# Four attention layers over eight batches on one core: last layers put beside the fronts of two batches on, and the two ends paired

## The reference, cut to what matters

```python
# layer 0: self-attention over pixels through 32 latent channels, then attention to 128 concepts
th, ph, g = conv1x1(x, w_theta), conv1x1(x, w_phi), conv1x1(x, w_g)         # 32 x 1024 each
sa_out = gamma_sa * conv1x1(softmax(th.T @ ph) @ g, w_o) + x
out0 = gamma_moca * conv1x1(softmax(conv1x1(sa_out, w_theta).T @ concepts.T) @ concepts, w_o) + sa_out
# layer 1: q and k of 32 channels, v of 256
out1 = softmax(q.T @ k) @ v * gamma + out0
# layer 2: group norm, q, k, v of 256 channels, one head
out2 = proj(softmax(q.T @ k / 16) @ v) + out1
# layer 3: group norm, q, k, v of 256 channels, 8 heads of 32, layer norm over channels at the end
out3 = layer_norm(wo(softmax(q.T @ k / sqrt(32)) @ v)) * ln_gamma + ln_beta + out2
```

## Time and profile before

| | us |
|---|---|
| median of 3 runs | 3100.76 |
| the profiled execution | 3099.89 |
| its span, first to last instruction | 3097.8 |
| TensorE matmul busy | 2771.0 (89%) |
| VectorE busy | 1812.1 (58%) |
| ScalarE busy | 1214.4 (39%) |
| GpSimd busy | 917.7 (30%) |
| mean granted TensorE clock | 0.885 of 2.4 GHz |

### The profile page before, as it was taken

The page is one execution under the profiler, slowest core; times in us unless marked ns, Lnnn a source line. Parts: engine busy times, 40 slices in busy tenths (PEclk is TensorE's granted clock), DMA queues, the critical chain, the costliest instruction groups (busy, mean ns, idle before and its releaser), DMA issues.

```text
span 3097.8 us, 25573 instructions
## 1 busy us (share of the span) xinstructions
PE 2771.0 (89%) x9636; PEld 1420.5 (46%) x9636; DVE 1812.1 (58%) x1749; ACT 1214.4 (39%) x2073; POOL 917.7 (30%) x371
## 2 busy tenths in 40 slices
PE   6788999989999899988999899898999989998877
PEld 3345445544354444544445444554435444454332
DVE  3233668357673766547675475835767376653675
ACT  2222262533435243442525335253343524344146
POOL 0111071502525034330515106150152503434045
PEclk7789898988989888997989989898898988899678
DMA  1002020020100201001010202002010020100300
GB/s 53 14 0 53 2 55 1 1 68 14 41 1 11 58 14 41 1 28 41 14 41 1 68 1 55 1 1 68 14 41 1 10 59 1 41 1 29 73 8 14
DMA packets 30347, 80.44 MB, mean 26 GB/s; under 512 B 10320, under 2 KB 10448, under 8 KB 28944
## 3 DMA queue, kind: packets, MB, share of 16 engines
q1 hardware_dynamic: 28048, 70.42, 9.0%
q0 software_dynamic: 2176, 8.39, 0.8%
HBM read 11.40 MB, written 8.39 MB: 6 GB/s over the span
## 4 chain that ended last, share of the span: by engine, by line
PE 70%; DVE 16%; ACT 5%; SPq 4%; issue 2%; POOL 1%; DMA 1%; DVEq 0%; ACTq 0%; POOLq 0%
PE ps L696 13%; PE ps L549 12%; PE ps L582 9%; PE ps L568 8%; DVE nmx_b L1218 8%; PE ps L863 7%; PE ps L781 6%; SPq L406 4%; DVE accb L1380 3%; PE ps L557 3%; PE ps L638 2%; PE ps L767 2%; PE ps L778 1%; POOL accb L499 1%; PE ps L678 1%
## 5 line engine op out<-in xcount | busy, mean ns | idle before, releaser
L1082 ACT ACTIVATE prb<-ps 128x512 f32<-128x512 f32 x1024 | 561.5, 599 | 452.1 <-PE ps L582 387.9
L1218 DVE TENSOR_REDUCE nmx_b<-ps 128x1 f32<-128x1024 f32 x512 | 605.6, 1216 | 102.7 <-PE ps L568 100.6
L499 POOL TENSOR_TENSOR accb<-accb,prb 128x1024 f32<-128x1024 f32 x192 | 503.3, 2621 | 247.6 <-ACT prb L1082 242.3
L568 PE MATMUL ps<-ks,qs 96*128 96x512 f32 x960 | 441.7, 570 | 118.8 <-DVE nmx_b L1218 74.6
L1380 DVE TENSOR_TENSOR accb<-accb,prb 128x1024 f32<-128x1024 f32 x192 | 396.2, 2063 | 259.5 <-ACT prb L1082 255.4
L499 POOL TENSOR_TENSOR accb<-prb 128x1024 f32<-128x1024 f32 x32 | 96.9, 3029 | 1484.7 <-ACT prb L1082 1404.2
L696 PE MATMUL ps<-pr,h 128*128 128x512 f32 x1024 | 482.7, 596 | 1.0 <-ACT tmp L978 1.0
L582 PE MATMUL ps<-qs,ks 97*128 97x512 f32 x960 | 388.0, 472 | 10.8 <-ACT prb L1082 7.8
L568 PEld LDWEIGHTS ps<-ks,qs 96*128 96x128 f32 x960 | 206.4, 246 | 322.5 <-DVE nmx_b L1218 222.8
L950 ACT ACTIVATE pr<-ps 128x512 f32<-128x512 f32 x384 | 226.7, 599 | 218.5 <-PE ps L582 104.0
L582 PEld LDWEIGHTS ps<-qs,ks 97*128 97x128 f32 x960 | 173.0, 192 | 251.9 <-ACT prb L1082 123.4
(11 more groups left out here) (157 smaller groups left out, 2714.0 us busy)
## 6 DMA issues: line engine op xcount, KB each, us to landing
qs<-part SPq DMA_DIRECT2D x180, 128.0 KB, 2.3
ks<-part SPq DMA_DIRECT2D x180, 128.0 KB, 2.3
x_in<-in_x POOLq DMA_DIRECT2D x8, 1024.0 KB, 5.3
xd<-xm SPq DMA_DIRECT2D x8, 1024.0 KB, 4.7
out<-prb SPq DMA_DIRECT2D x32, 256.0 KB, 2.0
q2k<-part SPq DMA_DIRECT2D x24, 128.0 KB, 2.3
w<-in_weights SPq DMA_DIRECT2D x1, 2592.0 KB, 10.0
qs<-nmx_rb SPq DMA_DIRECT2D x60, 4.0 KB, 1.7
```

The costliest lines, as they stand in the source:

```text
L499: pool.tensor_tensor(accb[:, 2:4, :], prb[:, (s - 1) % 2, 2:4, :] if j == 1 else accb[:, 2:4, :], prb[:, s % 2, 2:4, :], ALU.add)\
L568: mm = pe.matmul(ps[:, bank + jc, :], queries[0:STACK, tile(it)], keys[0:STACK, cols(jc)], start=True, stop=True)
L1082: act.activation(prb[:, s % 2, g, :], ps[:, turn3[score_use(s, g) % 3], :], ACT.Exp)\
L1218: dve.tensor_reduce(nmx[side][:, head, it:it + 1], ps[:, bank:bank + 2, :], AX.XY, ALU.max, negate=True).then_inc(max_sb[n].sem, 1)
```

## The change

- `batches` becomes three parts: front 0 beside front 1 ("fronts"), then six stages "both" with front b+2 beside back b, then back 6 beside back 7 ("backs"). `ORDER` has new lists for all three; the rule for the last back (`last`, `stacks3`, `both_rounds(..., last)`) is gone, and every back takes its rounds one after the other.
- Each side is now a **lane**, a set of tiles, PSUM banks and semaphores. Front 1 runs in the back's tiles and banks 4 to 7; back 7 runs in the front's tiles and banks 0 to 3, with the values in `xm[2]` and the sums of weights in the columns of `w` that only fronts use. `part` is still one tile, so backs 6 and 7 hand it to each other by waits on `stacked`.
- There are three tiles `xm`, used in turn by batch, in place of `x_in`, `xm` and `xd`. x is loaded straight into `xm[b % 3]`, layer 0 adds to it in place, and the final norm reads it. The copy to `xd` (1 MB in each stage) and the waits on it are gone.
- The first three batches are loaded by the SP queue behind the weights. The x of batch b+3 is loaded by SP in the tail of back b, after that back's last read of `xm` (`l3_g`, 4) and between its two pairs of stores; the front that needs it is the first work of the next stage.
- The ones in row 96 of the keys come by a small DMA once for each lane, in place of a VectorE memset of 4096 columns in the setup and a GpSimd memset before the last back. Many semaphores are put together into one with running counts.

The diff, cut to its core (bodies that only have `o.` put before their names are left out):

```diff
 def batches(engine, front, back):
-    finish(front(0))
-    for b in range(B - 1):
-        finish(merged("both", engine, front(b + 1), back(b)))
-    finish(back(B - 1))
-
-def both_rounds(engine, maxima, middle, steps, last):
-    yield from maxima(0)
-    yield from middle(0)
-    if last:
-        yield from merged("last", engine, steps(0), maxima(1))
-    else:
-        yield from steps(0)
-        yield from maxima(1)
-    yield from middle(1)
-    yield from steps(1)
+    finish(merged("fronts", engine, front(0), front(1)))
+    for b in range(B - 2):
+        finish(merged("both", engine, front(b + 2), back(b)))
+    finish(merged("backs", engine, back(B - 2), back(B - 1)))
+
+def both_rounds(maxima, middle, steps):
+    for u in range(CH):
+        yield from maxima(u)
+        yield from middle(u)
+        yield from steps(u)
...
-        x_in = sb("x_in", [P, CH, T])
-        xm = sb("xm", [P, CH, T])
+        xm = [sb(f"xm{n}", [P, CH, T]) for n in range(3)]
...
-        xd = sb("xd", [P, CH, T])
...
+        fronts = (
+            front_lane("fa", [0] + list(range(2, B)), 0, h, [q2k2[:, 2 * n:2 * n + 2, :] for n in range(4)], ks01[:],
+                       vgo[:], pr[:], acc[:], rden[:], tmp[:]),
+            front_lane("fb", [1], 4, hb[:], [qs[:, 0:2, :], qs[:, 2:4, :], ks[:, 0:2, :], ks[:, 2:4, :]], part[:, 0, :],
+                       vb[:, :, 0:2 * L], prb[:, 0, :, :], accb[:, 0:2, :], rdenb[:], accb[:, 2:4, :]))
+        backs = (
+            back_lane("ba", list(range(B - 1)), 4, hb[:], qs[:], ks[:], vb[:],
+                      [[prb[:, n, 2 * pair:2 * pair + 2, :] for pair in range(2)] for n in range(2)],
+                      [accb[:, 2 * pair:2 * pair + 2, :] for pair in range(2)], rdenb[:]),
+            back_lane("bb", [B - 1], 0, h[:], q2k2[:, 0:QUAD, :], q2k2[:, QUAD:, :], tokens(xm[B % 3]),
+                      [[pr[:, 0:2, :], pr[:, 2:4, :]], [acc[:], tmp[:]]],
+                      [w[:, pair, 0:2 * IW].rearrange("p (i n) -> p i n", i=2) for pair in range(2)], rden[:]))
...
+            for b in range(3):
+                sp.dma_start(xm[b][:], x_v[b]).then_inc(x_loaded[b].sem, 16)
...
+                def stacks(b, u):
+                    if u:
+                        sp.wait_ge(o.scored[3].sem, o.scored[3].at(b, QUAD * STEPS3))
+                    for done, src, dst, rows in ((o.q_hi, 0, o.queries, (0, 2)), (o.q_lo, 1, o.queries, (1,)),
+                                                 (o.k_hi, 2, o.keys, (0, 1)), (o.k_lo, 3, o.keys, (2,))):
                         sp.wait_ge(done[3].sem, done[3].at(b, IC * (u + 1)))
+                        if src == u == 0 and b == o.turns[0]:
+                            row = o.keys[ROW:ROW + 1, :, :].rearrange("p g (n c) -> p (g n) c", c=P)
+                            sp.dma_start(bf32(row), ones[0:QUAD * NT, :]).then_inc(o.ones.sem, 16)
...
-            def back(b):
-                last = b == B - 1
-                sp.wait_ge(res[2].sem, res[2].at(b, 4))
-                sp.dma_start(xd[:], xm[:]).then_inc(xd_copied.sem, 16)
-                yield
...
+                    for ic in range(IC):
+                        if ic and b + 3 < B:
+                            sp.wait_ge(o.l3_g.sem, o.l3_g.at(b, 4))
+                            sp.dma_start(xm[b % 3][:], x_v[b + 3]).then_inc(x_loaded[b % 3].sem, 16)
+                        for ch in range(CH):
+                            sp.wait_ge(o.l3_out.sem, o.l3_out.at(b, CH * ic + ch + 1))
+                            sp.dma_start(out_v[b, :, ch, cols(ic)], y(o, ch, ic)).then_inc(o.stored.sem, 16)
+                        yield
...
 @block.scalar
+                    if b == B - 1:
+                        act.wait_ge(backs[0].stacked[0].sem, backs[0].stacked[0].at(B - 2, 16 * 6 * QUAD))
+                    yield from queries_and_keys(0)
...
                             act.wait_ge(o.stacked[0].sem, o.stacked[0].at(b, 16 * 6 * QUAD))
+                            if b == B - 2:
+                                act.wait_ge(backs[1].stacked[0].sem, backs[1].stacked[0].at(B - 1, 16 * 6 * QUAD))
+                            if b == B - 1:
+                                act.wait_ge(backs[0].stacked[1].sem, backs[0].stacked[1].at(B - 2, 16 * 6 * QUAD))
                             yield from queries_and_keys(1)
...
 @block.vector
-            dve.memset(bf32(ks[ROW:ROW + 1, :, :]), 1.0).then_inc(setup_dve.sem, 1)
-            dve.memset(bf32(ks01[ROW:ROW + 1, :]), 1.0).then_inc(setup_dve.sem, 1)
+            for o in fronts:
+                dve.memset(bf32(o.ks01[ROW:ROW + 1, :]), 1.0).then_inc(setup_dve.sem, 1)
...
```

More of the change, by code:

```diff
@@ new lines, in tokens, with lane, in_turn @@
+        def tokens(ap):
+            return ap.rearrange("p h (n c) -> p (h n) c", c=C)
+        def lane(name, turns, bank):
+            o = Lane(name, turns, bank)
+            o.ps = ps[:, bank:bank + 4, :]
+            def in_turn(kind, counts):
+                sem, total = semaphore(f"{name}_{kind}"), sum(counts.values())
+                found, before = {}, 0
+                for key, count in counts.items():
+                    found[key] = Signal(sem, turns, total, before)
+                    before += count
+                return found
+            return o, in_turn
@@ L325, in score_use, with front_of, back_of, weights3 @@
+        def front_of(b):
+            return fronts[b == 1]
+        def back_of(b):
+            return backs[b == B - 1]
+        def weights3(o, s, g):
+            return o.pairs[s % 2][g // 2][:, g % 2, :]
+        def y(o, ch, ic):
+            return o.pairs[0][ch][:, ic, :]
+        def sq(o, ch, ic):
+            return o.pairs[1][ch][:, ic, :]
         def score_use(s, g):
@@ L379, in _ @@
             sp.dma_start(cst[:], constants).then_inc(loaded.sem, 16)
-            def front(b):
-                yield from ()
-            def shift_rows(b, u, last):
-                queries = stacks3(u, last)[0]
-                sp.wait_ge(max_r[3].sem, max_r[3].at(b, u + 1))
-                for q in range(QUAD):
-                    row = queries[ROW:ROW + 1, :, :].rearrange("p g (i q c) -> p q (g i) c", q=QUAD, c=L)
-                    sp.dma_start(bf32(row[:, q, :, :]), bf32(nmx_r["back"][L * q:L * q + L, :])).then_inc(shift_in.sem, 16)
-                yield
@@ L393, in stacks @@
-            def stacks(b, u, last):
-                queries, keys, _ = stacks3(u, last)
-                if u and not last:
-                    sp.wait_ge(scored[3].sem, scored[3].at(b, QUAD * STEPS3))
-                for done, src, dst, rows in ((q_hi, 0, queries, (0, 2)), (q_lo, 1, queries, (1,)),
-                                             (k_hi, 2, keys, (0, 1)), (k_lo, 3, keys, (2,))):
-                    if u == 0 or last:
-                        sp.wait_ge(done[3].sem, done[3].at(b, IC * (u + 1)))
-                    for r in rows:
-                        for g in range(QUAD):
-                            sp.dma_start(bf32(dst[L * r:L * r + L, g, :]),
-                                         bf32(part[L * g:L * g + L, src, :])).then_inc(stacked[u].sem, 16)
-                        yield
@@ L429, in _ @@
+            batches("SP", lambda b: program(front_of(b))[0](b), lambda b: program(back_of(b))[1](b))
+            for o in backs:
+                sp.wait_ge(o.stored.sem, o.stored.at(o.turns[-1], 16 * 4))
         @block.gpsimd
@@ L544, in _, with program, project @@
             pe.wait_ge(setup_dve.sem, SETUP_DVE)
[L546 to L555 removed]
+            def program(o):
+                def project(bank, name, src, m0, m, ic):
@@ L914, in _ @@
+                return front, back
+            batches("PE", lambda b: program(front_of(b))[0](b), lambda b: program(back_of(b))[1](b))
         @block.scalar
```

1768 lines of the change are left out of this document (893 added, 875 removed), and 41 rows, old and new, of the table ORDER.

## The result

The changed kernel takes 3000.03 us (median of four runs, 2999.77 to 3000.55). The kernel before, run beside it, takes 3102.28 us (four runs, 3092.09 to 3109.03). The ratio is 0.967, with a 95% interval from 0.965 to 0.970: 102 us less. The forecast was 3030 us, in a range of 2960 to 3085, with a chance of 0.83 for faster. Sign and range were right, and the time was 30 us too high.

The account below looks back on a forecast made before the run. TensorE looked like the bound, once its granted clock is counted, with 499 us of thinly filled lone ends; VectorE holds paired backs. Setup 22.8 + fronts 380 + stages 2220 + backs 405 = 3027.8, plus 2.1 outside: 3030 us, range 2960 to 3085.

Parts of the forecast that it names:

- Steps (1) to (4): Pair of backs: start 31.7 us, back 6's maxima alone 41.7, second queries and keys 11.0, its steps beside back 7's maxima 74.
- (5): Pair of backs: hand-over of `part` and second-round stacks, 24 DMAs then projections, 12 us counted as exposed.
- (7): Pair of backs: second hand-over of `part`, with eight maxima left to cover it, 10 us.
- (6): Pair of backs: steps of back 7 beside maxima of back 6, 74 us.
- (8): Pair of backs: steps 0 to 9 of back 6 beside 32 maxima, 57 us of VectorE time.
- (9): Pair of backs: thirteen steps of both backs in turn, no maxima, VectorE and GpSimd adds stretching each other, 47 us.
- (10): Pair of backs: steps 9 to 15 of back 7 at 3.9 us each, 27 us with its start.
- (11): Pair of backs: the end, 20.3 us.
- rival (a): Both pairs: gaps filled, TensorE keeps its high clock; fronts 350, backs 375, x hidden, 2955 us in all; chance 0.10.
- (b): Both pairs: chains don't interleave; fronts only 409, backs 440, stages 2220, 3094 us in all, no tellable change; chance 0.09.
- (c): Staging-buffer rival, pair of backs: single `part` and SP queue force turns; backs 510, 3135 us; chance 0.07 with (d).
- (d): Both pairs: lanes run in turn, not as the change says; fronts 500, 3150 us; chance 0.07 with (c).

Follow-up runs that it names:

- The copies above: Changed kernel with VectorE, in backs 6 and 7 alone, copying the newest weights to its sums where it added them: 2975.49 us, ratio 0.959.

## Why the prediction was right, and where it was off

**Setup**: right in size (21.6 for 22.8).

**Pair of fronts, 375.2 for 380**: right, step by step. The layers of the two lie as follows:

```profile
21.60:115.00 93.40, 85.16 (x286) 42.80 (x286) 45.63 (x46) 37.78 (x54) 0.00 (x0) 0.85 0.00 1
115.00:225.00 110.00, 105.29 (x282) 53.55 (x281) 49.14 (x57) 35.95 (x59) 34.64 (x16) 0.92 0.00 0
225.00:396.80 171.80, 169.92 (x572) 105.71 (x570) 49.03 (x69) 43.01 (x71) 33.19 (x16) 1.00 0.00 1
```

I cut them at round times near the layers' ends. Layers 0 and 1 take 203.4, forecast 197 and 7 for seams; layer 2 takes 171.8, forecast 176 at a rate of 0.97. The rate is 0.99: TensorE is busy for 169.9 of the 171.8 us at a granted clock of 1.00. Pricing by work (busy time times clock) and a rate from the densest mixed stretch held to 5 us where averages of whole stages would have given 409.

**Six stages, 2186.7 for 2220**: this is the step that failed. It said "the lists are re-cut, but the step counts and tiles are those of before, so 6 x 367.5 = 2205". The same steps in another order proved to be worth 5.7 us a stage where nothing else moves (the kernel before with the new lists), 34 us for six. The text priced new lists for the two pairs by reading them step by step, and took the third list on trust. The text had noted a loose stretch where maxima meet layer 0 (0.68 of full rate), but nothing was won there; the gain came in the stretch behind it, where TensorE was already busy for 0.96 of the time at a clock of 0.93, and most of it as less busy time at a clock of 1.00. So the rows of before did not show it plainly; what the sum lacked is a term of its own for the new order, with a lower end. The term for the copy was right: nothing (the same time with it put back). The term for the late load was right in size, 15 us forecast and 13.6 measured in the stages, but partly by luck: it stood for a wait of 2.5 to 3.5 us, and the wait that the load adds is 1.6; a lower clock supplies the rest. The prediction's own test, that it is wrong if the stages differ from 367.5 by more than 6 us, would have passed at 361.8 and at 364.45; it was too wide for a term that counts six times, and what it let pass is the whole miss.

**Pair of backs, 414.9 for 405**: about right in sum, by luck: its errors offset each other. The parts, in the columns of the stage view:

```profile
2583.50:2616.50 33.00, 25.11 (x71) 14.88 (x72) 12.83 (x34) 6.96 (x11) 0.00 (x0) 0.75 0.40 90
2616.50:2666.70 50.20, 44.04 (x103) 23.98 (x101) 41.35 (x38) 3.45 (x5) 0.00 (x0) 0.64 0.30 67
2666.70:2678.00 11.30, 10.33 (x26) 4.84 (x25) 7.71 (x11) 3.29 (x6) 0.00 (x0) 0.94 0.01 1
2678.00:2742.20 64.20, 57.36 (x259) 24.18 (x259) 55.54 (x43) 36.28 (x69) 41.00 (x14) 0.90 0.17 39
2742.20:2753.90 11.70, 10.79 (x22) 4.81 (x22) 5.16 (x9) 3.27 (x5) 0.00 (x0) 0.82 0.29 63
2753.90:2812.50 58.60, 51.06 (x252) 21.07 (x251) 54.42 (x38) 35.85 (x68) 42.03 (x14) 0.96 0.11 25
2812.50:2824.30 11.80, 10.88 (x23) 5.29 (x20) 10.15 (x10) 1.23 (x2) 0.00 (x0) 0.50 0.65 146
2824.30:2881.80 57.50, 50.60 (x195) 23.28 (x194) 50.74 (x44) 25.39 (x47) 20.11 (x8) 0.82 0.00 1
2881.80:2924.40 42.60, 36.68 (x156) 13.15 (x157) 34.28 (x15) 28.39 (x55) 33.45 (x12) 0.79 0.00 1
2924.40:2975.80 51.40, 41.34 (x152) 13.42 (x152) 29.35 (x18) 29.03 (x53) 25.85 (x9) 0.80 0.06 21
2975.80:2998.40 22.60, 11.91 (x27) 4.99 (x24) 6.29 (x9) 11.70 (x18) 0.00 (x0) 0.80 0.12 46
```

- Steps (1) to (4), start, first maxima, second projections, steps beside maxima: 158.7, forecast 31.7 + 41.7 + 11 + 74 = 158.4. Inside, work sits otherwise than priced: the maxima of back 6 take 50.2 and not 41.7, since projections of back 7 run among them, and the mixed stretch takes 64.2 and not 74, since it holds 28 of the maxima of back 7 and not 32.
- Steps (5) and (7), the hand-overs of `part`: 11.7 and 11.8, forecast 12 and 10. Here the staging-buffer rival would have stood at 27 us or more. ScalarE's high part does wait for stacks there (5.9 us at the first one), as the prediction said it would show. Neither takes 20 us.
- Step (6): 58.6, forecast 74. The stretch was priced with 32 maxima, while the list gives it 24 and the prediction itself kept eight for step (7): 23 ran in it. Nine maxima at 1217 ns are 11 of the 15 us. This is a slip in the count, to be found in the prediction's own text.
- Step (8): 57.5, forecast 57 from VectorE's time alone. The length fits, but not by that sum: VectorE was busy for 50.7 of it, since its nine adds took 1.6 us each (14.4 in all) and not 2.1.
- Steps (9) and (10), both backs without maxima: 94.0, forecast 47 + 27 = 74. There were 21 steps (85 exponentials, four a step) where I had counted 20: all 16 of back 7 lie behind its last maxima, and steps 7 and 8 of it fell between my (9) and (10), while one step of back 6 too many stood in (9). So one step takes 4.5 us, not 3.6 to 3.9. The contention was named rightly, and the end of back 6 (its output projection and norm on VectorE, which the sum didn't price) lies in it too. The two lines of that stretch that carry it are

```profile
L1446 DVE TENSOR_TENSOR w<-w,pr 128x1024 f32<-128x1024 f32 x6 | 15.3, 2550 | 0.6 <-ACT pr L1138 0.4
...
L555 POOL TENSOR_TENSOR w<-w,pr 128x1024 f32<-128x1024 f32 x6 | 18.6, 3102 | 7.6 <-ACT pr L1138 7.4
```

VectorE's add takes 2550 ns for 1.21 us undisturbed, GpSimd's 3102 for 2.35. With GpSimd's adds of back 7 on VectorE, the same stretch takes 77.9. So the way of adding costs 16 us here, most of the 20 by which the forecast was short; that the price per step was short for this reason alone isn't shown, since that kernel also has fewer waits between two engines.

- Step (11): 22.6, forecast 20.3.

**The range's ends.** The dense pairs of rival (a), 350 and 375, weren't reached by either pair (375.2 and 414.9), though the kernel came within 45 us of its 2955, by the stages. Rivals (b), (c) and (d) are out: the pairs interleave, the hand-overs are short, and the lanes don't run in turn, which costs 113.6 and 132.0 us when it is forced.

## What to carry to other kernels

A hand-made order of several engines is a term of the sum of its own, even where every step count stays: give the term a size and a lower end, measure it apart from the rest of the change (the old and the new order in both kernels), and don't take one engine's part of a new order without the others'. Ends that run alone are worth pairing when their chains leave TensorE idle; price the pair by work (busy time times granted clock) and by the rate of the densest mixed stretch, then count the steps of each stretch from the list, each once. A load at a seam can cost more than what it lands late (1.6 us of wait became 2.7 to 3.4 us a stage here): halves of it, each started at the last read of that half, took the whole cost away.

## What the runs showed of the hardware

VectorE and GpSimd stretch each other also when VectorE reads only one operand from SBUF. The copies above take 0.70 us alone and up to 2.87 beside GpSimd's adds, VectorE's adds 1.21 and up to 3.47: in both cases up to 2.2 or 2.3 us more, nearly a whole GpSimd add. The prediction had weighed only the case of two inputs, and its contrast with the reduction, which reads PSUM and stayed at means of 1213 to 1220 ns in every stretch looked at, was right but not the whole of it. The Trainium skill, SBUF — State Buffer, section "SBUF: two separate sides", puts the pair of ports under an exclusive lock that is held for a whole instruction, by a GpSimd operation or by a VectorE one with two SBUF inputs or in a 2-port mode. By the Trainium skill, VectorE: DVE Perf Modes, section "Mode 2×_2P — use both read ports for one tensor", an fp32 copy inside SBUF can run in such a mode. The traces agree with both: the copy takes 0.70 us where the add takes 1.21, and what a collision adds, up to 2.3 us, is about one whole instruction of GpSimd (2.35).

The loads from HBM landed 5.6 us after issue for 1 MB and 4.2 us for 512 KB, so half the data spares a quarter of the time. The second half started at the same place as the whole load had, so it is its size that made it early enough: it landed 0.2 us before the first projection.
